# Letting the first score maxima of a rope group stand beside the last key tile of the rope group two places earlier

## The reference

```python
# branch "rope": keys and queries from 64 latent features, plus a rotary part of 64 features
scores = (einsum('bhtd,bhsd->bhts', q, k) + einsum('bhtd,bsd->bhts', qr, kr)) * scale
attn = softmax(where(causal, scores, -inf));  out = (attn @ v) @ Wo
# branch "shared": one key and one value for all heads, chosen by a top-1 router
att = softmax(where(causal, einsum('bhqd,bkd->bhqk', q, k_shared) * hd**-0.5, -inf)); y = att @ v_shared
```

## The kernel before

| place | units at its points | sum |
|---|---|---|
| (g-1, 0) | 2 1 0 1 1 1 | 6 |
| (g-1, 1) | 2 1 2 1 3 1 | 10 |
| (g-1, 2) | 1 1 2 1 3 1 | 9 |
| (g-1, 3) | 1 1 2 1 2 0 | 7 |
| (g-1, 4) | 1 2 3 | 6 |

## Time and profile before

### The profile page before, as it was taken

One profiled execution on the slowest core, in us unless ns is written; L12 is line 12 of the kernel. 1 busy time (PEld: TensorE's weight loads), 2 busy tenths in 40 slices (PEclk: granted clock), 3 DMA queues, 4 the chain that ended last, 5 costly groups with the idle time before them and its releaser, 6 DMA issues.

```text
span 928.1 us, 12052 instructions
## 1 busy us (share of the span) xinstructions
PE 840.9 (91%) x4835; PEld 497.8 (54%) x4835; DVE 562.2 (61%) x999; ACT 386.6 (42%) x477; POOL 236.5 (25%) x211
## 2 busy tenths in 40 slices
PE   8998999999899999996899998679999889989997
PEld 3554453445354435444478794523333258888776
DVE  3878658774876678216443553577778326964552
ACT  2641345346444645563523402115556763510240
POOL 4641322421142114513321101400111137710110
PEclk8979999999999999998889997769999989999999
DMA  6464069315731850204000004949000061000001
GB/s 187 77 198 124 23 147 162 90 70 86 119 81 68 140 142 1 77 1 152 8 1 1 1 3 152 126 104 121 2 1 1 1 237 47 0 1 1 0 1 46
DMA packets 35584, 64.99 MB, mean 70 GB/s; under 512 B 6164, under 2 KB 14908, under 8 KB 35460
## 3 DMA queue, kind: packets, MB, share of 16 engines
q1 hardware_dynamic: 34952, 64.08, 29.7%
q10 hardware_dynamic: 576, 0.13, 0.1%
HBM read 44.35 MB, written 16.29 MB: 65 GB/s over the span
## 4 chain that ended last, share of the span: by engine, by line
PE 65%; DVE 19%; ACT 5%; DMA 4%; SPq 3%; issue 2%; POOL 2%; ACTq 0%; DVEq 0%; POOLq 0%
PE psD L1808 11%; PE psO L1946 11%; PE psA L1808 10%; PE psD L1891 9%; PE psA L1909 8%; DVE mx L1384 8%; PE psO L1808 7%; PE psA L1908 3%; SPq L604 3%; PE psD L1893 2%; ACT Pr L1054 2%; DVE hid_low L1704 1%; DMA Ks<-in_c_ones4b 1%; PE psD L1960 1%; POOL Pr L905 1%
## 5 line engine op out<-in xcount | busy, mean ns | idle before, releaser
L1384 DVE TENSOR_REDUCE mx<-psD 128x1 f32<-128x512 f32 (+3 forms) x418 | 258.4, 657 | 89.1 <-PE psD L1893 63.7
L1054 ACT ACTIVATE Pr<-psA 128x1024 f32<-128x1024 f32 (+3 forms) x192 | 161.8, 866 | 161.7 <-PE psA L1909 161.3
L905 POOL TENSOR_SCALAR_AFFINE_SELECT Pr<-Pr 128x512 f32<-128x512 f32 x96 | 61.1, 637 | 385.5 <-ACT Pr L1054 309.8
L1059 ACT ACTIVATE Pr<-psA 128x1024 f32<-128x1024 f32 (+3 forms) x96 | 63.6, 703 | 60.6 <-PE psA L1909 60.3
L1946 PE MATMUL psO<-Pr,Vh 128*32 128x512 f32 (+3 forms) x768 | 80.8, 500 | 3.1 <-POOL Pr L905 2.5
L1908 PE MATMUL psA<-Qr,Kr 128*128 128x512 f32 (+3 forms) x192 | 75.0, 404 | 0.7 <-ACT xnT L1014 0.7
L1893 PE MATMUL psD<-maskq,identb 128*128 128x128 bf16 x350 | 70.8, 227 | 0.0
L1909 PE MATMUL psA<-Qr,Kr 113*128 113x512 f32 (+3 forms) x192 | 65.8, 349 | 0.0
L1891 PE MATMUL psD<-Kg,Qs 96*128 96x512 bf16 (+3 forms) x192 | 54.9, 334 | 7.8 <-DVE mx L1384 4.9
L1891 PE MATMUL psD<-Kr,Qr 80*128 80x512 bf16 (+3 forms) x166 | 50.6, 347 | 7.0 <-DVE mx L1384 6.1
L1891 PE MATMUL psD<-Ks,Qs 96*128 96x512 bf16 (+3 forms) x166 | 51.5, 354 | 4.7 <-DVE mx L1384 3.7
(11 more groups left out here) (420 smaller groups left out, 1684.3 us busy)
## 6 DMA issues: line engine op xcount, KB each, us to landing
Qr<-d_qr SPq DMA_DIRECT2D x18, 512.0 KB, 11.6
d_qr<-WB SPq DMA_DIRECT2D x9, 512.0 KB, 3.5
Pr<-d_cb SPq DMA_DIRECT2D x8, 512.0 KB, 7.0
Qs<-d_gq SPq DMA_DIRECT2D x24, 128.0 KB, 4.1
Qs<-d_q SPq DMA_DIRECT2D x24, 128.0 KB
Ks<-d_k SPq DMA_DIRECT2D x24, 128.0 KB
Qr<-d_qn SPq DMA_DIRECT2D x18, 128.0 KB, 7.2
Kr<-d_kn SPq DMA_DIRECT2D x18, 128.0 KB, 7.9
```

The costliest lines, as they stand in the source:

```text
L905: pool.affine_select(out=block_, in_=block_, pattern=[[0, GH], [1, P]], compare_op=ALU.is_ge, fill=0.0, base=0, channel_multiplier=-1).the ...
L1054: act.activation(place[:, h, q0:T], src[:, q0:T], ACT.Exp, scale=score_scale(i)).then_inc(a_drained, 1)
L1059: act.activation(place[:, h:h + 2, q0:T], src[:, :, q0 - HALF:HALF], ACT.Exp, scale=score_scale(i)).then_inc(a_drained, 1)
L1384: dve.tensor_reduce(mx[:, j, part, h0:h0 + nh], src, AX, ALU.max).then_inc(d_drained, 1)
```

## The change

`max_window` is widened for rope groups: the one place (g-2, 7), the last key tile of the rope group two places earlier, comes ahead of (g-1, 0) to (g-1, 4). In `paced` a break is added: at that place only units with j below 4 may be taken, those that need the first half of the columns. Nothing is computed otherwise than before.

```diff
@@ -106,7 +106,7 @@ max_window
-    tail = [(i - 2, kt) for kt in range(max_end(i - 1), NT) if i - 2 >= first and not is_mla(i)]
+    tail = [(i - 2, kt) for kt in range(NT - 1 if is_mla(i) else max_end(i - 1), NT) if i - 2 >= first]
     return tail + [(i - 1, kt) for kt in range(max_end(i))]
@@ -188,6 +188,8 @@ paced
                 while (products or waiting.get(g)) and not (row and n == 0):
+                    if not products and g == i + 2 and is_mla(g) and waiting[g][0][0] >= NT // 2:
+                        break
                     if not pace.bank_free() and (n < len(points) - 1 if products else len(at) >= behind):
                         break
```

## The result

The changed kernel takes 1.0054 times as long as the kernel before, 95% interval 1.0035 to 1.0073, from 17 runs of each. On the 920.62 us of the kernel before that is +5.0 us (3.2 to 6.7). The forecast was +0.9 us, with 924.6 as the upper end of the range; 1.0054 x 920.62 is 925.6. It is slower, and by more than the range allowed.

What follows compares the result with a forecast made beforehand. TensorE was taken as the bound, with 65% of the chain. Stalls against relief gave -1.0 us and the clock +2.0, so +1.0 on 920.62, rounded to 921.5; range 918.0 to 924.6.

Steps and rivals of the forecast that it cites:

- The order of the units: Four units, 0 to 3, at each of (0, 7), (2, 7), (4, 7), at the points as 2 0 2.
- Step 1: Units moved to (g-2, 7): sum 0, but the second half of the columns lands 0.83 us later.
- Steps 2 and 4: Waits for column halves: stalls of 2.0 and 1.8 us in group 2, 2.2 in group 4, 1.4 in group 6.
- The overlap that was named among the rivals: In group 2, stall and fall overlap, since a slowed TensorE comes later to the second wait.
- Step 3: Group 4's maxima after the stall: 1.7 us back from fewer waits against 1.65 behind; gains 0.1 us.
- Step 5: Clock behind four new TensorE stalls: two falls at 1.0 us each, 2.0; bounds none, and four at 1.7, 6.8.
- the 0.6 that I let vanish: Of 1.7 us of work lost per fall, 0.6 vanishes in waits for VectorE and for the second half.
- three or four falls: Clock falls behind the new TensorE stalls, the case on the slower side; chance 0.23.
- The one on the slower side: Every stall is followed by a clock fall of 1.1 to 1.7 us: 924 to 926; chance 0.23.
- its turning point: The number of clock falls from which the slower rival decides: three.
- four falls, some 924.5: Sum by the skill page: matmul bursts cut by DMA waits fall to the slow clock at all four stalls.
- The rival that the waits for VectorE go and nothing replaces them: Second half lands before TensorE comes; relief 2.4 us a group, time 915; no stall, chance 0.12.

Runs made afterwards that it cites:

- e2: Changed kernel's wider window for groups 4 and 6 alone, group 2 in the old order; 1.0014 against the kernel before.
- e4: Changed kernel with ten discarded matmuls ahead of the wait for group 2's first half; 1.0033 against the kernel before.
- e9: Changed kernel with discarded matmuls ahead of all four new waits (group 2's first half, unit 11 of groups 2, 4, 6); 1.0000 against the kernel before.
- e3: Kernel before, old order, but TensorE waits for group 2's first half in (0, 7) as the changed kernel does; 1.0030 against the kernel before.
- e10: Kernel before with e3's wait and ten discarded matmuls ahead of it; 1.0008 against the kernel before.
- e1: Changed kernel's wider window for group 2 alone, groups 4 and 6 in the old order; 1.0035 against the kernel before.
- e11: Changed kernel, new load queue: early first half, group 3's operands behind group 2's loads, second half in two pieces; 0.9941 against the kernel before.
- e12: Kernel before, units in old order, with the load queue of e11; 0.9984 against the kernel before.
- e6: Kernel before, old order, with group 2's first half loaded ahead of group 3's operands; 1.0033 against the kernel before.
- e7: Changed kernel with group 2's first half ahead of group 3's operands and the second half in two pieces; 1.0021 against the kernel before.
- e8: Kernel before, old order, with the load queue of e7; 1.0051 against the kernel before.

## Why the prediction was wrong, point by point

**The order of the units** came as forecast: four at each of the three places, two of them ahead of the last scores. **Step 1** held: moved work gained nothing by itself, and group 4's second half is issued 0.85 us later behind the mark, against 0.83 forecast.

**Steps 2 and 4, where TensorE waits.** The place of the waits was right. The first was sized at 2.0 us and measured 2.31; group 4's at 2.2 and measured 1.40, 1.89 in e2 and 1.74 in e4; group 6's at 1.4 and measured 0.91, 1.19 and 1.45. Group 2's second wait, forecast at 1.8, doesn't exist in the changed kernel, since TensorE at half clock comes to unit 11 after the load; with the clock held in e4 it is there, 1.34 us. The overlap that was named among the rivals is what happened. In group 4 the load landed 15.6 us behind the mark, against 15.7 forecast; TensorE was there at 14.2, against 13.5, which is the shorter stall.

**Step 3, what comes back.** The sum of stall and relief was forecast at -0.1 for groups 2 and 4 and -0.8 for group 6, -1.0 together. Without falls (e9) it is +0.9, 0.0 and +0.2, +1.1 together, and the runs say 0.0 us (-1.3 to 1.3). Group 6's unit 11 comes 0.4 us later in e9 than in the changed kernel, which has no fall there either and shows -0.2. So group 2 lost 0.9 where a gain of 0.1 was forecast, and group 6 gained 0.2 where 0.8 was. This is off by 1 to 2 us of the 4 that were missed.

**Step 5, the clock, is the step that failed.** It was taken as two falls of 3.4 us at 1.0 us each. The mechanism was right, and so was the number of falls in the profile; the size of one was not, neither its cost per 3.4 us nor its length. In all, 2.0 us were put down for the clock, and e9 against the changed kernel measures 5.0 (the two intervals lie apart). A fall of 3.4 us in a stretch costs 1.8 us in the changed kernel's group 4 (41.23 against 39.42), 1.6 by e3 against e10, and 2.2 in e4's group 4 (41.61 against 39.44 in e9): nearly the whole 1.7 us of lost work or more. So the 0.6 that I let vanish didn't vanish in a short fall. Why isn't shown; in the long fall of group 2 some did (half of 17.1 us is 8.6, and 5.7 were lost). And a fall doesn't always last 3.4 us. In group 2 it lasted 17.1 us, in e1 again, and cost 44.67 - 38.97 = 5.7 us. The rows that I went by showed 3.4 us alone. The same trace has twelve stretches at half clock besides the one at its very end, of 3.4 to 20.5 us, and only three of them are as short as 3.4. One of 10.2 us stands ahead of the attention, with TensorE busy all through it and no idle time over 0.2 us in the 5 us before it, which I didn't weigh:

```profile
45.70:56.00 10.30, 10.30 (x46) 7.38 (x46) 9.03 (x18) 3.56 (x2) 8.88 (x6) 0.50 0.76 150
```

**Which gaps bring a fall.** The prediction gave three or four falls 0.23. The fourteen profiles can be counted for this, from 91 to 400 us. All twelve idle times of TensorE from 1.39 to 4.29 us, each a wait for a load or for the row of maxima, had a fall that began within them or within 1.1 us behind. Of the 31 from 1.19 to 1.34 us three had one, and of those from 0.7 to 1.0 us none. By this count the forecast stalls of 2.0, 1.8, 2.2 and 1.4 us would all have had one; the changed kernel has three stalls, and that of 0.91 us had none. No run varied the length of a wait alone, so this is a count and not a limit.

**The rivals.** The one on the slower side, that the clock falls behind the stalls, is what happened, though not from three falls on as its turning point said: two were enough, one of them long. "By it the sum would be four falls, some 924.5", said of the Trainium skill, TensorE: Matmul & The Clock Gate, section HAM oscillation, was nearer than my own sum; this case's runs agree with the page that waits for DMA leave TensorE at the slow clock (0.50 for 17.1 us behind 2.31 us). But the count of four falls was my own inference: the page's example has waits of some 3 to 5 us, longer than any stall that was forecast here. The rival that the waits for VectorE go and nothing replaces them is no story of the changed kernel. With the loads in time it comes near: the wider window is then worth 4.0 us (e11 against e12) of the 5.7 that the rival had, since smaller waits do take the place of the old ones; the rest of e11's -5.4 us is the queue's own.

**What stays open.** Why the slow stretch lasts 17.1, 17.1, 13.7 and 10.2 us in the changed kernel, e1, e6 and e7, but 3.4 in e3 and e8. The first four don't share an order of units (e6 has the old one), and e8 has a longer wait (4.29 us) with a short fall. And the fall is an event of single executions: the gap of 1.2 us in group 3's places was followed by one in the kernel before and in e9, and by none in the other twelve profiles. What each timed run's mean clock tells is the sum over the whole kernel (the last column of the table): 16 us more at half clock in the changed kernel's runs, where its profile has 20.5 in the stretches. How that splits between groups, and how long each fall was, it doesn't tell.

## What to carry to other kernels

Before moving work to an earlier place, look up when its operands land and what trigger issues their load; a wait that the old order had hidden comes to light, and work put ahead of the trigger makes the load later still. Price a stall of the bounding engine not by its length but with the clock behind it: here three stalls of 0.9 to 2.3 us cost about as much as the relief of VectorE won, and the slow clock behind them 5 us. How long such a slow stretch may last is to be read from all of the trace, not from the two nearest ones. If the move is right and only the loads are late, mend the queue: the same order went from +5.0 to -5.4 us when the loads were cut and reordered. Look then at the small transfers on the critical path: twice here (e6, e8) a queue that was meant to change nothing made TensorE wait longer for the row of maxima, 2.18 and 4.29 us instead of 1.31.

## What the runs showed of the hardware

- Keeping TensorE busy with discarded matmuls through a wait for a load, whose end stays the same, kept the clock at 1.00: 38.97 against 44.67 us in one stretch, and 1.0000 against 1.0054 in the whole kernel.
- TensorE stayed at 0.50 for 17.1 us although it was busy 17.10 of 17.10 us in that window of the changed kernel, with mixed small and large matmuls. Stretches at half clock with TensorE busy all through or nearly so lasted 3.4 to 17.1 us here.
- In fourteen profiles, from 91 to 400 us, all twelve idle times of TensorE of 1.39 us and more had a fall of the clock at or just behind them, and three of the 31 from 1.19 to 1.34 us.
- An 8 KB transfer from ScalarE's queue took 5.37, 6.24, 7.99 or 8.34 us with bulk loads of SyncE's queue on the way beside it, in four orders; with the queue of e11 and e12, which issues the next load 1.7 us behind it, its last packet had ended after 1.4 us. The Trainium skill, DMA: Bandwidth & Descriptors, section Issuing engines are not separate DMA queues, says that transfers of all issuing engines interleave on the same DMA engines; these lengths agree.
